# Two Swin blocks on one NeuronCore: P out of a second, turned score product, and the queues ordered for it

## The reference, cut to what matters

```python
x = x.transpose(0, 2, 3, 1); shortcut = x
x = layer_norm(x, g1, b1); x = roll(x, (-4, -4))           # then windows of 8 x 8 = 64 tokens
q, k, v = split(x @ w_qkv + b_qkv)                          # 12 heads of 16
attn = softmax(q @ k.T * 16 ** -0.5 [+ rel_bias + mask])    # bias and mask in block 0 only
x = shortcut + roll((attn @ v) @ w_proj + b_proj, (4, 4))
x = x + gelu(layer_norm(x, g2, b2) @ w_fc1 + b_fc1) @ w_fc2 + b_fc2   # 768 hidden
```

## Time and profile before

| | us |
|---|---|
| median of 3 runs (lowest, highest) | 4842.09 (4838.08, 4854.21) |
| the profiled execution | 4850.49 |
| its span, first to last instruction | 4848.1 |
| TensorE busy | 4275.9 (88%) |
| Vector busy | 3373.7 (70%) |
| GpSimd busy | 2997.4 (62%) |
| ScalarE busy | 2773.6 (57%) |

### The profile page before, as it was taken

One profiled execution on the slowest core, in us unless ns is written; L12 is line 12 of the kernel. 1 busy time (PEld: TensorE's weight loads), 2 busy tenths in 40 slices (PEclk: granted clock), 3 DMA queues, 4 the chain that ended last, 5 costly groups with the idle time before them and its releaser, 6 DMA issues.

```text
span 4848.1 us, 175812 instructions
## 1 busy us (share of the span) xinstructions
PE 4275.9 (88%) x66384; PEld 3016.7 (62%) x66384; DVE 3373.7 (70%) x9081; ACT 2773.6 (57%) x5921; POOL 2997.4 (62%) x6254
## 2 busy tenths in 40 slices
PE   4888888898899989898889898999888988898987
PEld 2566666666666666666666666666666666666665
DVE  5666676667677767776667776777776777677765
ACT  1555555556566556565556555656555555565654
POOL 4666666666666666666566666666665666666654
PEclk9999999999999999999999999999999999999999
DMA  4445444444444544444444454444454444444543
GB/s 95 84 84 88 82 88 89 87 82 88 89 89 88 93 86 89 92 87 86 86 88 87 87 91 88 87 91 89 87 88 85 87 87 89 87 86 88 88 81 58
DMA packets 1560580, 420.58 MB, mean 87 GB/s; under 512 B 1457462, under 2 KB 1558202, under 8 KB 1559740
## 3 DMA queue, kind: packets, MB, share of 16 engines
q1 hardware_dynamic: 1559740, 409.35, 46.3%
HBM read 31.56 MB, written 25.17 MB: 12 GB/s over the span
## 4 chain that ended last, share of the span: by engine, by line
PE 45%; DMA 13%; POOL 10%; issue 10%; DVE 9%; SPq 9%; ACT 2%; DVEq 0%; POOLq 0%; ACTq 0%
PE ps_s L569 12%; DMA qkt<-qk 9%; PE bank L581 8%; PE bank L448 6%; PE bank L543 4%; POOL hid L1098 4%; DVE smax L893 3%; SPq L356 3%; SPq L371 3%; PE ps_t L526 2%; PE ps_s L515 2%; DVE hid L931 2%; POOL xs L1091 2%; DMA ht<-xs 2%; PE ps_s L506 2%
## 5 line engine op out<-in xcount | busy, mean ns | idle before, releaser
L1036 POOL TENSOR_TENSOR rstd<-vare,half 128x2 f32<-128x2 f32 x518 | 359.1, 693 | 1138.1 <-DVE vare L871 1138.1
L931 DVE TENSOR_TENSOR hid<-hid 128x512 f16<-128x512 f32 x768 | 600.6, 782 | 511.5 <-POOL hid L1098 491.4
L569 PE MATMUL ps_s<-ht,w_fc 128*128 128x512 f16 x3840 | 879.8, 382 | 18.6 <-DMA ht<-xs 10.1
L581 PE MATMUL bank<-w_fc,hid 128*128 128x192 f16 x9216 | 851.8, 247 | 7.5 <-DVE hid L931 5.5
L581 PEld LDWEIGHTS bank<-w_fc,hid 128*128 128x128 f16 x9216 | 774.6, 98 | 80.5 <-issue 53.2
L893 DVE TENSOR_REDUCE smax<-ps_s 128x12 bf16<-128x768 f32 x512 | 488.2, 954 | 453.3 <-PE ps_s L506 442.8
L683 ACT ACTIVATE pt<-ps_t 128x768 f16<-128x768 f32 x512 | 414.8, 810 | 598.7 <-PE ps_t L526 595.6
L1098 POOL TENSOR_SCALAR hid<-hid 128x512 f16<-128x512 f32 x768 | 561.8, 732 | 297.0 <-ACT hid L691 295.9
L691 ACT ACTIVATE hid<-ps_s,b_fc 128x512 f32<-128x512 f32 x768 | 529.6, 690 | 333.8 <-PE ps_s L569 158.6
L569 PEld LDWEIGHTS ps_s<-ht,w_fc 128*128 128x128 f16 x3840 | 361.1, 98 | 464.0 <-issue 69.5
L448 PE MATMUL bank<-w_qkv,xt 128*128 128x384 f16 x2560 | 530.5, 340 | 25.0 <-DMA xt<-xs 23.2
(11 more groups left out here) (113 smaller groups left out, 7420.9 us busy)
## 6 DMA issues: line engine op xcount, KB each, us to landing
x_img<-in_x_dram SPq DMA_DIRECT2D x256, 96.0 KB, 2.2
out_dram<-y_img SPq DMA_DIRECT2D x256, 96.0 KB, 1.9
xt<-xs SPq DMA_TRANSPOSE x512
qkt<-qk SPq DMA_TRANSPOSE x512, 3.9
ot<-os SPq DMA_TRANSPOSE x512, 2.4
ht<-xs SPq DMA_TRANSPOSE x512, 2.3
stage<-in_L_conv_fc_w_dram SPq DMA_DIRECT2D x2, 384.0 KB, 4.2
stage<-in_L_conv_w_fc_dram SPq DMA_DIRECT2D x2, 384.0 KB, 3.9
```

What stands on the lines that cost most here:

```text
L569: last = mm(ps_s[:, u % 2, :], w_fc1[layer][:, part, m * 128:(m + 1) * 128], ht[:, p % 2, blk, :], start=(i == 0), stop=(i == 4))
L581: mm(bank[:, 0:C], hid16[:, hs, m, tok], w_fc2[layer][:, ws, m, :], start=(m == 0 and i == 0), stop=False)
L931: v.tensor_tensor(hid16[:, 1, m, :], hid[:, u % 2, :], hid16[:, 0, m, :], ALU.subtract)\
```

## The change

Five things change at once.

1. `p_transpose` is gone. A new step `scores_turned` computes the scores a second time with the operands swapped, keys on partitions, straight into ps_t; block 0's bias goes in by a second pass. `shift_scores` now subtracts the maximum there, 12 matmuls with the broadcast maximum as weights. `exp` reads ps_t, writes `p_exp`; `p_hi` and `p_lo` read that.
2. `hidden` pieces use four banks (0, 1, 4, 5 in ps_s, 2 and 3 in ps_t), `hid` has four buffers, the waits reach four pieces back. Pieces 0 and 1 are in place 0, 2 to 5 in place 1.
3. `projection` writes ps_tr in place of ps_qk, and takes turns there with x_transpose and y_transpose.
4. `scores` waits for the maximum of the tile before, not for its exp.
5. Every engine's order in a slot is new.

The core of the diff (`...` stands for parts of a line left out; comments on the right name the function or the queue):

```diff
-        p_tok = sb("p_tok", [128, 2, PAIRS, 2, WIN], F32)
+        p_exp = sb("p_exp", [128, 2, PAIRS * TOK], F32)
-        hid = sb("hid", [128, 2, GROUP * TOK], F32)
+        hid = sb("hid", [128, 4, GROUP * TOK], F32)
+        def hidden_bank(m):
+            return (ps_s, ps_t)[m // 2 % 2][:, m % 2, :]
 # sync
-                    ge("s_mm", n - 2)                      # qk_turn
+                    ge("t_mm", n - 2)
-                if live(s + 1):
-                    qk_turn(s + 1)
+                if live(s - 1):
+                    o_turn(s - 1)
                 if live(s + 3):
                     norm1_turn(s + 3)
                 if live(s - 3):
                     norm2_turn(s - 3)
-                if live(s - 1):
-                    o_turn(s - 1)
-                (load of tile s + 9, store of s - 9 / s - 13)
+                if live(s + 2):
+                    qk_turn(s + 2)
+                (load of tile s + 7, store of s - 10 / s - 14)
 # tensor
-                    if n < 5:                              # qk_product
-                        ge("qk_lo", n - 1)
-                    ge("resid1", n - 5)
+                    ge("qk_lo", n - 1)
-                    ge("exp_done", n - 1)                  # scores
+                    ge("max_done", n - 1)
+                def scores_turned(n):
+                    _, layer, t = visit(n)
+                    ge("exp_done", n - 1)
+                    if layer == 0:
+                        for g in range(PAIRS):
+                            for par in range(2):
+                                mm(ps_t[par * 64:par * 64 + 64, g // 3, g % 3 * TOK:(g % 3 + 1) * TOK],
+                                   bias_tab[:, par, g, :], pair_ident[:, :],
+                                   start=(g % 3 == 0), stop=False, skip_group_check=True)
+                    else:
+                        pe.nop(nofuse=True)
+                    for g in range(PAIRS):
+                        for w in range(2):
+                            for par in range(2):
+                                rows = slice(par * 64, par * 64 + 64)
+                                tok = slice(w * WIN, (w + 1) * WIN)
+                                place = g % 3 * TOK + w * WIN
+                                last = mm(ps_t[rows, g // 3, place:place + WIN],
+                                          qkt[rows, n % 2, PAIRS + g, tok], qkt[rows, n % 2, g, tok],
+                                          start=(layer == 1 and g % 3 == 0 and w == 0), ...)
+                    last.then_inc(S["t_mm"], 1)
                 def shift_scores(n):
                     ge("max_done", n)
-                    for par in range(2):
-                        last = mm(ps_s[:, par, 0:PAIRS * WIN]..., neg_ident[:, :],
-                                  smax[:, n % 2, par, :].unsqueeze(2).broadcast_to([128, PAIRS, WIN]), ...)
+                    for g in range(PAIRS):
+                        for par in range(2):
+                            last = mm(ps_t[par * 64:par * 64 + 64, g // 3, g % 3 * TOK:(g % 3 + 1) * TOK],
+                                      smax[:, n % 2, par, g:g + 1].broadcast_to([128, WIN]), neg_ident[:, :], ...)
-                def p_transpose(n):
-                    ge("p_lo", n - 1)
-                    ge("exp_done", n)
-                    for g in range(PAIRS):
-                        last = nc.tensor.transpose(ps_t[...], p_tok[:, n % 2, g]..., ident[:, :])
-                    last.then_inc(S["tp"], 1)
-                    if live(n + 4):                        # projection
-                        ge("qk_lo", n + 4)
-                    else:
-                        ge("resid1", n - 1)
+                    take_tr("resid1", n)
-                    contract(ps_qk[:, 0:C], w_proj[layer], ...)
+                    contract(ps_tr[:, 0:C], w_proj[layer], ...)
-                        ge("exp_done", min(s, ENDS))       # hidden
-                    if m >= 2:
-                        ge("gelu", u - 2)
+                        ge("max_done", min(s, ENDS))
+                    if m == 2:
+                        ge("exp_done", min(s - 1, ENDS))
+                    if m >= 4:
+                        ge("gelu", u - 4)
 # scalar
+                    ge("p_lo", n - 2)                      # exp
-                    nc.scalar.activation(p_tok[...], ps_s[...], ACT.Exp)
+                    nc.scalar.activation(p_exp[...], ps_t[:, :, 0:3 * TOK], ACT.Exp)
-                    ge("tp", n)                            # p_hi
-                    copy(pt[:, n % 2, 0]..., ps_t[:, :, 0:3 * TOK], ACT.Copy)
+                    ge("exp_done", n)
+                    copy(pt[:, n % 2, 0]..., p_exp[:, n % 2], ACT.Copy)
-                    ge("h_lo", u - 2)                      # gelu
+                    ge("h_lo", u - 4)
 # vector
-                    v.tensor_tensor(pt[:, n % 2, 1]..., ps_t[:, :, 0:3 * TOK], pt[:, n % 2, 0]..., ALU.subtract)
+                    v.tensor_tensor(pt[:, n % 2, 1]..., p_exp[:, n % 2], pt[:, n % 2, 0]..., ALU.subtract)
-                    residual(n, ps_qk[:, 0:C], stream(n, 1), stream(n, 0), "pr", "resid1")
+                    residual(n, ps_tr[:, 0:C], stream(n, 1), stream(n, 0), "pr", "resid1")
```

More of the change, by code:

```diff
@@ L225, in swin_program @@
             "centred rstd bn1a bn1 ln1 hi1 lo1 qk_mm v_mm mask_set qk_hi qk_lo v_hi v_lo "
-            "s_mm max_done shift exp_done tp p_hi p_lo pv inv_done o_norm o_hi o_lo "
+            "s_mm t_mm max_done shift exp_done p_hi p_lo pv inv_done o_norm o_hi o_lo "
             "pr resid1 bn2a bn2 ln2 hi2 lo2 fc2 resid2".split(), TOTAL)
@@ L260, in run @@
         def run(slot):
-            for s in range(-4, TOTAL + GROUP + 9):
+            for s in range(-4, TOTAL + GROUP + 10):
                 slot(s)
@@ L595, in slot @@
                 mlp = 0 <= p < PHASES
+                last_block = mlp and visit(p * GROUP)[1] == 1
                 if mlp and place == 1:
-                    hidden(4)
-                    hidden(5)
-                if live(s + 4) and visit(s + 4)[1] == 0:
-                    x_transpose(s + 4)
+                    for m in range(2, HC):
+                        hidden(m)
+                if mlp and place == 2:
+                    ge("o_norm", min(s - 2, ENDS))
+                    mlp_out(p * GROUP + 1, ps_o)
+                if mlp and place == 3:
+                    if last_block:
+                        y_transpose(p * GROUP)
+                    ge("v_lo", min(s - 1, ENDS))
+                    if s - 1 > ENDS:
+                        ge("resid2", p * GROUP)
+                    mlp_out(p * GROUP + 2, ps_v)
                 if live(s - 3):
@@ L948, in slot @@
                 if live(s):
                     row_max(s)
+                if mlp and place == 1:
+                    hidden_lo(4)
+                    hidden_lo(5)
+                if live(s):
                     v_lo(s)
-                if mlp and place == 1:
-                    hidden_lo(5)
-                if live(s + 3):
-                    mean_variance(s + 3, 0)
+                if live(s - 1):
+                    inverse_sums(s - 1)
+                    o_norm(s - 1)
                 if live(s - 3):
+                    statistics(s - 3, 1)
@@ L969, in slot @@
-                if mlp and place > 0:
-                    mlp_residual(p * GROUP + (0, 0, 2, 3)[place], ps_v)
-                if live(s + 4):
-                    statistics(s + 4, 0)
             run(slot)
@@ L1103, in slot @@
                 if live(s + 2):
+                    apply1(s + 2)
+                if mlp and place == 1:
+                    for m in range(3):
+                        hidden_hi(m)
+                if live(s + 2):
+                    full1(s + 2)
                     norm1_lo(s + 2)
                 if mlp and place == 1:
+                    hidden_hi(3)
                     hidden_hi(4)
```

161 lines of the change are left out of this document (76 added, 85 removed).

## The result

| | us |
|---|---|
| median after, 4 runs (lowest, highest) | 5038.97 (5027.64, 5045.25) |
| median before, in the same job | 4845.24 |
| ratio, 95% interval | 1.0396 (1.0368, 1.0424): slower |
| profiled execution after, its span | 5027.64, 5025.9 |

What follows compares the result with a forecast made beforehand. TensorE's work, 31.4 us of a 36.8 us phase, leaves stalls, mostly scores waiting for qkt. Slots laid end to end gave 35.4: −1.4 x 128 = −180 us from 4850.5, 4670, less 8, stated as 4660; range 4400 to 4860.

Steps and rivals of the forecast that it cites:

- TensorE's sum is even, only stall can be gained: TensorE's work per phase: 31.6 us after the change, no less than before; any gain must come from stalls.
- Columns one by one: Rival on TensorE: second scores 0.65, shift and bias 0.64, 2.0 a phase; 4830 to 4860 us, chance 0.09.
- Bound (b), Q/K of the next slot at S+8.0: Q/K waits for xt, issued 5.6 us after shift start S and landing in 2.4, so starts no earlier than S+8.0.
- o_turn went into the idle time ahead: SyncE's row: ot's transpose moves ahead of xt, so xt to qkt issue takes 3.2 us instead of 5.8.
- xt chain: Rival: Vector's new order puts xt 1.2 us later, its landing slower; phase 37.8, 4970 us, chance 0.14.
- The slots: Shift-to-shift times laid end to end by place: mean phase 35.4 us against 36.8.
- the 4660: Forecast median time in us of the likeliest case, chance 0.45, its own range 4560 to 4740.
- The waits that go: TensorE's waits after: row maximum under 20 us, scores' qkt wait below 150 of 292.
- The ps_tr wait: TensorE's wait for the bank projection now shares; over 50 us would show the forecast wrong.
- SyncE's gap from xt to qkt, 3.2: On SyncE, issue of xt to issue of qkt: near 3.2 us, was 5.8.
- The port, 0.45 beside p_lo: p_lo's two SBUF inputs delay GpSimd's xt chain 0.45 us; as a rival 0.95, 4790 us, chance 0.17.
- The range and the chances: 4400 to 4860 us, leaving out the xt case and far ends of others; faster 0.75, same 0.07, slower 0.18.

Runs made afterwards that it cites:

- Run 10: Changed kernel with xt transposed from the tile before's xs (wrong values) and first on SyncE, ahead of ot: 4833.2 us, ratio 0.9979.
- run 2: Changed kernel with p_lo's float32 operand read from ps_t in PSUM instead of SBUF (low part not the wanted one): 4940.3 us, ratio 1.0214.
- 9: Kernel before with second scores and split shift in its old order, p_lo's operand from PSUM banks at rest (wrong low part): 5020.4 us, ratio 1.0371.
- run 11: Changed kernel with xt from the tile before's xs, first on SyncE, and p_lo's operand from ps_t (wrong values): 4772.6 us, ratio 0.9857.
- 3: Kernel before with second scores and split shift replacing the P transposes, old order, p_lo reading P from SBUF: 5106.6 us, ratio 1.0550.
- run 1: Changed kernel with Vector's statistics and centre ahead of reciprocal and norm, GpSimd's scale and apply2 ahead of o_hi and o_lo: 5095.3 us, ratio 1.0538.
- 5: Changed kernel with p_lo moved on Vector to the next slot, ahead of the row maximum: 5174.9 us, ratio 1.0662.
- 6: Changed kernel with Vector's centre ahead of reciprocal and norm, o_hi and o_lo a slot later, ot behind qkt on SyncE: 5130.0 us, ratio 1.0569.
- 7: Changed kernel with the edits of 6 and p_lo ahead of the row maximum: 5171.7 us, ratio 1.0656.
- 8: Kernel before with second scores in its old order, p_hi at ScalarE's head and p_lo ahead of the row maximum: 5121.6 us, ratio 1.0557.

## Why the prediction was wrong

- **TensorE's sum is even, only stall can be gained**: right. Second scores and shift, start to start in the slot above, 0.50 (forecast 0.45, though its own 24 x 20 ns make 0.48) and 0.44 (0.44). No gap shows at the mode switches; a drain of a few hundredths of a us inside these start-to-start times would not show. "Columns one by one" is out: 24 second-score matmuls in 0.50 are 21 ns each, not 27.
- **Bound (b), Q/K of the next slot at S+8.0**: this is the step that failed, by the size of its terms. It was xt's issue at S+5.6 plus a landing of 2.4, the median of ot. The landing was too short: where TensorE waited for xt, it started a mean 3.0 to 4.2 us after xt's issue, by place, and 3.4 over all 283 waits. In place 3 the issue was as forecast (5.5), and the whole miss, 8.9 for 8.0, is this. In place 1 it is this and the issue: 10.1 and 10.5 where the sum had 9.3 and 8.9. There layer 0's centre ends at S+3.7, not 2.9; I had made layer 0 earlier than layer 1 (3.3), and it is later. Run 10 prices the lateness: 206 us.
- **"o_turn went into the idle time ahead"**: true of the rows of places 0, 1 and 3, false of place 2, where the late row pushes xt to 0.6 to 1.2 us behind its low part. Little waits for that xt.
- **The rival "xt chain"** (phase 37.8; measured 38.2), which I gave 0.14, has the mechanism and nearly the time, but the time in part by luck. The measured bounds lie between mine and its own (place 1: 9.3, measured 10.1 to 10.5, 11.2; place 3: 8.0, measured 8.9, 10.0), and its condition, a landing of 3.6, was met only for xt of places 0 and 2. The slot with the hidden pieces makes up the rest.
- **The slots.** Shift to shift, in us, layer 1 / layer 0:

| slot | forecast | changed kernel | run 10, without the xt wait |
|---|---|---|---|
| place 0 (hidden pieces) | 12.0 / 11.8 | 13.6 / 13.2 | 12.7 / 12.8 |
| place 1 | 7.7 / 8.6 | 7.7 / 8.6 | 7.7 / 8.6 |
| place 2 | 8.4 / 8.0 | 9.6 / 9.2 | 8.3 / 8.2 |
| place 3 | 6.5 / 7.8 | 7.2 / 7.7 | 7.5 / 7.8 |

- Place 2 is lost to xt and comes back without it. Place 0 does not: it lies 0.7 and 1.0 us over the forecast with no wait for xt left, some 105 us of the run, and run 10 as a whole is 173 us above the 4660. In layer 0 the x transpose waits 1.0 us a slot there for the residual, on the bank that the projection now shares; what else fills it stays open.
- **The waits that go.** Shift: right, 20 us (forecast under 20). The ps_tr wait: 44.7, inside the 50 allowed, but 61 in run 10. qkt: wrong. 167 is over the 150 named, and with xt out of the way it is 326. The sign did not follow from the sum: laid end to end its own slots stand for qkt 1.4 and 0.7 us in layer 1 and 1.3 and 1.1 in layer 0, 288 us in all. The gain was to come from shorter slots, not from this wait. The banks are neutral, sharing ps_tr a gain.
- **SyncE's gap from xt to qkt, 3.2**: right, the median is 3.4.
- **The port, 0.45 beside p_lo**: not so in any place. From the end of centre to that of xt's low part it is 3.7 us in place 1 and 3.2 in places 2 and 3, and without the port (run 2) 3.15 and 3.2. So it cost 0.6 where the longest xt waits are and under 0.1 elsewhere, and xt's 5.5 in place 3 came out right only because the port's 0.45 was not there and small things on the way made up for it. p_lo itself hardly varied (944/960/1126); what was stretched was GpSimd's scale, to a mean of 842 and at most 1406 ns, and the norms. Its worth is 86 to 98 us (runs 2, 9), 61 once xt is off the chain (run 11). The Trainium skill, SBUF — State Buffer, Who interferes with whom, says that a Vector instruction with two SBUF inputs contends with a GpSimd instruction that reads SBUF, and that the shared ports are an exclusive lock; runs 3 and 9 agree, the scale's 1261 ns were 692 again with one operand from PSUM.
- **The range and the chances**: 4400 to 4860 left out the very rival whose threshold I had computed. The slot shown in the rows had xt 4.4 us from issue to use; with xt 1.2 us later in every slot there was nothing left to spare, and I put 2.4, a median of another transpose, in the sum of the likeliest case. The kernel before had the number: its 34 waits for xt end a mean 3.8 us after the issue.

## What to carry to other kernels

In a loop over several engines, one late item in a serial queue can set the period, and removing its wait may only uncover the next one (here xt hid qkt, and ht hid the mask). So lay out every item's ready time in the queue's order before moving any, by place in the pattern and not by a median over all, and ask of each who stands behind it. A landing time in such a sum must be that transfer's own. Test a suspected dependence by making it ready early with the same instructions in place (old data); that gave 206 us in one run where five reorderings on suspicion (1, 5, 6, 7, 8) all lost. A tiny producer behind long work on its engine (0.23 us of mask) can cost more than anything the busy shares show: moving it gained 277 us.

## What the runs showed of the hardware that I had not expected

- A Vector instruction of two float32 columns (`nmean`) took 169 ns in the median before and 523 after, standing beside GpSimd's `o_lo`; it fell back to 170 when both moved (run 1). A tiny instruction can be stretched threefold like this; that the shared port is the cause here was not tested:

```profile
L889 DVE TENSOR_SCALAR nmean<-mv x518: 158/523/549, 77.3 to 4996.5; 128x2 f32<-128x2 f32 x173
```

- `exp` in place in PSUM (128x768, float32) takes 783/795/795 ns, from PSUM into SBUF 782/810/813: no price for writing PSUM shows. The high part read from PSUM takes 810 where it took 843 from SBUF.
